# Attention scores of two units at once, computed from 64 rows each, in a sparse-attention, Mamba and FFN kernel

## The reference

```
scores = einsum('bhqd,bhkd->bhqk', Q, K) * scale
mask   = causal & ((cols >= rows - 31) | ((rows - cols) % 64 == 0))
out    = einsum('bhqk,bhkd->bhqd', softmax(where(mask, scores, -inf)), V)
```

## Time and profile before

| | us |
|---|---|
| Median of 3 runs (809.6 to 815.29) | 811.17 |
| The profiled execution | 811.52 |
| Its span, from first to last instruction | 809.7 |
| TensorE busy | 721.4 (89%) |
| VectorE busy | 695.3 (86%) |
| GpSimd busy | 664.2 (82%) |
| ScalarE busy | 594.8 (73%) |

### The profile page before, as it was taken

The page is one execution under the profiler, slowest core; times in us unless marked ns, Lnnn a source line. Parts: engine busy times, 40 slices in busy tenths (PEclk is TensorE's granted clock), DMA queues, the critical chain, the costliest instruction groups (busy, mean ns, idle before and its releaser), DMA issues. The chain is left out here.

```text
span 809.7 us, 22189 instructions
## 1 busy us (share of the span) xinstructions
PE 721.4 (89%) x7840; PEld 430.6 (53%) x7840; DVE 695.3 (86%) x1187; ACT 594.8 (73%) x1161; POOL 664.2 (82%) x824
## 2 busy tenths in 40 slices
PE   5999988998789999998999999899896889897887
PEld 3765655644455447545555456355452356453566
DVE  6977229999999989999889999999998989799983
ACT  5776698797788989887689978868667744764533
POOL 5143437998899989989999799899998999999961
PEclk9999999999999999999999999999999999998999
DMA  5000019888799668877777889889797899898950
GB/s 200 3 3 2 2 54 269 226 231 229 206 225 237 159 173 238 230 177 200 198 213 197 225 233 243 232 230 244 207 253 199 252 259 240 215 266 235 264 158 27
DMA packets 84177, 154.94 MB, mean 191 GB/s; under 512 B 9433, under 2 KB 10082, under 8 KB 84066
## 3 DMA queue, kind: packets, MB, share of 16 engines
q1 hardware_dynamic: 84066, 153.51, 71.4%
HBM read 142.46 MB, written 11.01 MB: 190 GB/s over the span
## 5 line engine op out<-in xcount | busy, mean ns | idle before, releaser
L1779 POOL TENSOR_TENSOR d<-d,cr 128x1024 f32<-128x1024 f32 x128 | 300.0, 2354 | 13.8 <-DVE d L1279 4.1
L1578 ACT ACTIVATE ps<-dt,An 128x512 f32<-128x512 f32 x256 | 173.7, 690 | 71.9 <-DVE d L1279 60.5
L1279 DVE TENSOR_TENSOR_SCAN d<-ps,hl,d 128x512 f32<-128x512 f32 x128 | 157.0, 1262 | 3.7 <-ACT ps L1578 3.3
L1279 DVE TENSOR_TENSOR_SCAN d<-ps,d 128x512 f32<-128x512 f32 x128 | 149.6, 1202 | 7.2 <-ACT ps L1578 6.5
L1267 DVE TENSOR_TENSOR d<-ps,d 128x512 f32<-128x512 f32 x184 | 118.5, 671 | 7.1 <-DMA d<-dud 7.1
L891 PE MATMUL ps<-h,w 128*128 128x512 f16 (+1 forms) x512 | 114.3, 373 | 3.5 <-DVE h L1224 2.8
L1766 POOL TENSOR_TENSOR d<-d,br 128x512 f32<-128x512 f32 x72 | 91.5, 1277 | 4.3 <-DMA d<-dud 4.3
L891 PEld LDWEIGHTS ps<-h,w 128*128 128x128 f16 x512 | 46.8, 98 | 70.9 <-DVE h L1224 12.8
L966 PE MATMUL ps<-d,cst 128*32 128x512 f32 x512 | 69.3, 614 | 10.6 <-POOL d L1779 6.4
L1434 ACT COPY pt<-ps 128x512 f32<-128x512 f32 x96 | 53.8, 589 | 13.9 <-PE ps L825 10.6
L825 PE MATMUL ps<-cst,sx 128*128 128x128 f32 x384 | 56.3, 281 | 8.0 <-ACT sx L1427 3.5
(11 more groups left out here) (182 smaller groups left out, 1457.1 us busy)
## 6 DMA issues: line engine op xcount, KB each, us to landing
dt<-dtd SPq DMA_DIRECT2D x256, 256.0 KB, 5.3
d<-dud SPq DMA_DIRECT2D x256, 256.0 KB, 4.8
dtd<-sR SPq DMA_DIRECT2D x16, 256.0 KB, 4.4
dud<-sE SPq DMA_DIRECT2D x16, 256.0 KB, 3.8
X<-in_x SPq DMA_DIRECT2D x8, 256.0 KB, 6.3
br<-bcd SPq DMA_DIRECT2D x8, 256.0 KB
cr<-bcd SPq DMA_DIRECT2D x8, 256.0 KB
out<-X SPq DMA_DIRECT2D x3, 512.0 KB, 5.8
```

The lines of the kernel that those rows point to most:

```text
L1279: eng.tensor_tensor_scan(d, banks[u % NG][:, :], d, hl[:, r:r + 1] if m % 2 else 0.0, ALU.mult, ALU.add).then_inc(v_sc, 1)
L1578: eng.activation(banks[u % NG][:, :], DT[:, u % NT, :], ACT.Exp, scale=An[:, g:g + 1]).then_inc(s_da, 1)
L1779: eng.tensor_tensor(d, d, CR[m % 2][:, :].unsqueeze(1).to_broadcast((128, n, 512)), ALU.mult).then_inc(p_cm, n)
```

## The change

- A far unit is now 8 windows by 8 heads (64 channels) instead of 4 windows by 16 heads. `UNITS` gets a fourth entry `c`, the half of the channels; the number of units stays 24. Far scores are made in pairs as near ones were: `asc_t` runs for even units only and takes two banks.
- A far pair is 32 products of 64 rows by 64 weight columns that stream 64 columns (8 windows, 2 halves `c`, 2 column halves `j`). A near pair is 8 products of 64 rows by 128 weight columns that stream 128 columns, where it was 16 of 64 by 64.
- Each mask product is made from 64 rows: `e4` becomes the sum of two 32-column pieces of the identity, so that each half of its rows holds what all 128 held.
- `KD` holds two copies instead of four, masked by `rmask` (1 where `row // 32 % 2` is the copy's number). They are written by two 128-row operations with a per-row factor instead of four 32-row copies. GpSimd zeroes only the 64 columns of padding, and `vz_p` no longer touches `KD`.
- `ZF`, `apv_t`, `afar_v`, `aown_s`, `asb_t` and `asc_v` follow the new shape of the far unit, with the same numbers of instructions and elements.
- `WARM` has 42 entries with 215 products, where it had 28 with 152. Two entries of 8 and 2 products stand ahead of the two first transposes. By places: below 100000, 13 products (0 before); 100000 to 280000, 56 (14); to 440000, none (none); to 600000, 20 (21); above, 126 (117).
- `PLACES` is new throughout, so the order of all engines changes.

The diff, without the places and without lines that only follow from the new fourth entry of `UNITS`:

```diff
@@ -21,7 +21,7 @@
 
 
 CONST, NCONST = {}, 0
-for _name, _n in (("ident", 128), ("qmask", 4), ("csel", 56), ("one8", 1)):
+for _name, _n in (("ident", 128), ("qmask", 4), ("csel", 56), ("one8", 1), ("rmask", 2)):
     CONST[_name] = (NCONST, _n)
     NCONST += _n
 
@@ -40,6 +40,7 @@
     put("ident", np.eye(128, dtype=np.float32))
     put("qmask", ((p[:, None] // 8 % 4 == np.arange(4)[None, :]) * float(HD) ** -0.5).astype(np.float32))
     put("csel", (np.arange(56)[None, :] == 24 + p[:, None] % 8).astype(np.float32))
+    put("rmask", (p[:, None] // 32 % 2 == np.arange(2)[None, :]).astype(np.float32))
     put("one8", (p == RK).astype(np.float32))
     return out
 
@@ -64,12 +65,7 @@
 
 
 GROUPS = [(1, g) for g in range(4)] + [(0, g) for g in range(4)]
-UNITS = [(kind, g, kk) for kind, g in GROUPS for kk in range(2 if kind else 4)]
-
-
-def near(u):
-
-    return (u - 8) % 4 // 2, u % 2
+UNITS = [(kind, g, kk, c) for kind, g in GROUPS for kk in range(1 if kind else 2) for c in range(2)]
 NU = len(UNITS)
 
 
@@ -149,7 +145,7 @@
     (BATCH_HALVES, 'aln_p aln_s aln_t ano_s aqk_s aqk_t'),
     (GROUPS_OF, 'afar_v aval_s aval_t'),
     (UNITS_OF, 'aown_s apv_t asc_s asc_v atr_s atr_t'),
-    ([(b, u) for b, u in UNITS_OF if u < 8 or u % 2 == 0], 'asc_t'),
+    ([(b, u) for b, u in UNITS_OF if u % 2 == 0], 'asc_t'),
     ([(b, u) for b, u in UNITS_OF if u in SHIFTED_T], 'asb_t'),
     (JOINS, 'aback_v jexp_s jmix_p jout_t jrec_v jsub_p jsum_p jtr_v jx_v'),
...
@@ -747,27 +742,26 @@
                                            aT[:, 64 * m + 32 * s:64 * m + 32 * s + 64], WT[:, 2, :], start=True, stop=True)
                 t.then_inc(t_av, 1)
 
-            def scores(b, u, mk):
-
-                U = NU * b + u
-                bank = bank_of["sc", b, u] = turn((s_exp, U + 1) if u in SHIFTED_T else (v_sub, shifted(b, u, "v") + 1))
-                eng.matmul(bank[:, :], e4[:, :], mk, start=True, stop=False, skip_group_check=True)
-                return bank
-
             def asc_t(b, u):
-                kind, g, kk = UNITS[u]
+
+                kind, g, kk, _ = UNITS[u]
                 U, gi = NU * b + u, group_of(u)
+                nw = 8 if kind else 4
                 if U == 0:
                     eng.wait_ge(v_set, V_SEL)
-                if kind:
-                    bank = scores(b, u, masks[:, 256:288].unsqueeze(1).to_broadcast((128, 16, 32)))
-                else:
-                    kk, _ = near(u)
-                    if g == kk == 0:
-                        mk = masks[:, 0:256].unsqueeze(1).to_broadcast((128, 2, 256))
+                half = [slice(64 * c, 64 * c + 64) for c in range(2)]
+                two = []
+                for c in range(2):
+                    by = (s_exp, U + c + 1) if u + c in SHIFTED_T else (v_sub, shifted(b, u + c, "v") + 1)
+                    bank = bank_of["sc", b, u + c] = turn(by)
+                    if kind:
+                        mk = masks[half[c], 256:288].unsqueeze(1).to_broadcast((64, 16, 32))
+                    elif g == kk == 0:
+                        mk = masks[half[c], 0:256].unsqueeze(1).to_broadcast((64, 2, 256))
                     else:
-                        mk = masks[:, 64:192].unsqueeze(1).to_broadcast((128, 4, 128))
-                    two = [scores(b, u + c, mk) for c in range(2)]
+                        mk = masks[half[c], 64:192].unsqueeze(1).to_broadcast((64, 4, 128))
+                    eng.matmul(bank[:, :], e4[half[c], :], mk, start=True, stop=False, skip_group_check=True)
+                    two.append(bank[:, :].rearrange("p (a w k) -> p a w k", a=2, w=nw))
                 if b == 0:
                     eng.wait_ge(v_aqm, gi + 1)
                 else:
@@ -775,45 +769,39 @@
                 eng.wait_ge(s_aqk, 4 * b + 2)
                 if U == 0:
                     eng.wait_ge(v_akd, 2)
+                if b == 0 and u == 8:
+                    eng.wait_ge(p_set, 2)
+                if kind == 0 and g == 2:
+                    eng.wait_ge(p_kp, b + 1)
                 qm = QM[gi % 2]
-                if kind:
-                    bw = bank[:, :].rearrange("p (a w k) -> p a w k", a=4, w=4)
-                    Ks = KD[:, :, PAD:PAD + T].rearrange("p a (h x) -> p a h x", x=128)
-                    for k in range(4):
-                        m = 8 * g + 4 * kk + k
-                        lq = qm[:, 4 * kk + k, :, :].rearrange("p a n -> p (a n)")
-                        t = eng.matmul(bw[:, :, k, :].rearrange("p a (h x) -> p a h x", x=4), lq, Ks[:, :, :, 4 * m:4 * m + 4], start=False,
-                                       stop=(k == 3 and u not in SHIFTED_T), skip_group_check=True)
-                    t.then_inc(t_sc, 1)
-                    return
-                if g == 2:
-                    eng.wait_ge(p_kp, b + 1)
-
-                for k in range(4):
-                    m = 8 * g + 4 * kk + k
-                    at = 64 * (m % 16) + m // 16
+                Ks = KD[:, :, PAD:PAD + T].rearrange("p a (h x) -> p a h x", x=128)
+                for k in range(nw):
+                    wi = nw * kk + k
+                    m = 8 * g + wi
                     for c in range(2):
-                        r = slice(64 * c, 64 * c + 64)
-                        for j in range(2):
-                            o = slice(64 * j, 64 * j + 64)
-                            lq = qm[r, 4 * kk + k, 2 * j:2 * j + 2, :].rearrange("p a n -> p (a n)")
-                            dst = two[c][o, :].rearrange("p (a w k) -> p a w k", a=2, w=4)[:, :, k, :]
-                            t = eng.matmul(dst, lq, KD[r, 2 * c:2 * c + 2, at:at + 127:2], start=False,
-                                           stop=(k == 3 and u + c not in SHIFTED_T), skip_group_check=True)
-                        if k == 3:
+                        end = k == nw - 1 and u + c not in SHIFTED_T
+                        if kind:
+                            for j in half:
+                                lq = qm[half[c], wi, j.start // 32:j.stop // 32, :].rearrange("p a n -> p (a n)")
+                                t = eng.matmul(two[c][j, :, k, :].rearrange("p a (h x) -> p a h x", x=4), lq, Ks[half[c], :, :, 4 * m:4 * m + 4],
+                                               start=False, stop=end, skip_group_check=True)
+                        else:
+                            at = 64 * (m % 16) + m // 16
+                            lq = qm[half[c], wi, :, :].rearrange("p a n -> p (a n)")
+                            t = eng.matmul(two[c][:, :, k, :], lq, KD[half[c], :, at:at + 127:2], start=False, stop=end, skip_group_check=True)
+                        if k == nw - 1:
                             t.then_inc(t_sc, 1)
 
...
             def atr_t(b, u):
@@ -826,26 +814,21 @@
                 t.then_inc(t_at, 1)
 
             def apv_t(b, u):
-                kind, g, kk = UNITS[u]
+                kind, g, kk, c = UNITS[u]
                 U, gi = NU * b + u, group_of(u)
+                nw = 8 if kind else 4
                 V, pt = (V1, V2)[kind][g % 2], PT[U % 2]
                 eng.wait_ge(s_av, 8 * b + gi + 1)
                 eng.wait_ge(s_pt, U + 1)
                 bank = bank_of["pv", b, u] = turn((s_own, U + 1))
-                if kind:
-                    bo = bank[:, 0:144].rearrange("p (w a n) -> p w a n", w=4, a=4)
-                    for a in range(4):
-                        for j in range(4):
-                            t = eng.matmul(bo[32 * j:32 * j + 32, :, a, :], pt[:, a, 32 * j:32 * j + 32], V[:, kk, :, 4 * a + j, :], start=True, stop=True)
-                else:
-
-                    kk, c = near(u)
-                    bo = bank[:, 0:72].rearrange("p (w a n) -> p w a n", w=4, a=2)
-                    for i in range(4):
-                        a, w = i // 2, i % 2
-                        for j in range(4):
-                            t = eng.matmul(bo[32 * j:32 * j + 32, 2 * w:2 * w + 2, a, :], pt[:, i, 32 * j:32 * j + 32],
-                                           V[:, 2 * kk + w, :, 4 * (2 * c + a) + j, :], start=True, stop=True)
+                bo = bank[:, 0:18 * nw].rearrange("p (w a n) -> p w a n", w=nw, a=2)
+
+                for i in range(4):
+                    a, w = i // 2, i % 2
+                    at = slice(nw // 2 * w, nw // 2 * w + nw // 2)
+                    for j in range(4):
+                        t = eng.matmul(bo[32 * j:32 * j + 32, at, a, :], pt[:, i, 32 * j:32 * j + 32],
+                                       V[:, 2 * kk + w, :, 4 * (2 * c + a) + j, :], start=True, stop=True)
                 t.then_inc(t_pv, 1)
 
             def jout_t(b, g):
...
@@ -1048,7 +1031,7 @@
             eng.tensor_copy(masks[:, :], mraw0).then_inc(v_set, 2)
             eng.wait_ge(l_w1, 16)
             for k in range(4):
-                eng.tensor_copy(e4[:, 32 * k:32 * k + 32], ident[:, 0:32]).then_inc(v_set, 2 if k == 3 else 1)
```

(20 more changed lines are left out.)

246 lines of the change are left out of this document (121 added, 125 removed), and 321 rows, old and new, of tables (PLACES, WARM).

## The result

The changed kernel takes **820.33 us** (median of 4 runs, 819.21 to 821.72) beside 810.5 us (4 runs) for the kernel before on the same chip: ratio 1.0098, 95% interval 1.0057 to 1.0138 (the quotient of the two medians is 1.012, inside that interval). The forecast was 802, the range ended at 817. The profiled execution took 819.21 us, its span is 817.4 (809.7 before), so the span grew by 7.7 us.

A forecast was written before the change was run, and what follows sets the result against it. It took TensorE to set the pace from 20 to 100 us, VectorE as nearest full to 640, GpSimd afterwards. 811.5 - 1.7 (start) - 3.7 (batch 0) - 3.5 (batches 1 to 3) - 0.4 (key copies) = 802.2, forecast 802; range 789 to 817.

The forecast's parts named there:

- Near scores: Near pairs on TensorE: two 64-row masks stream together, no gain in products; -0.21 us a pair, 32 pairs, -6.7 us.
- Far scores: Far pairs on TensorE: narrower products in quicker rounds, 1.5 us a pair; -0.7 us a pair, 16 pairs, -11.2 us.
- The start: Query and key products before the first scores: early idle products bring the faster clock sooner; -1.7 us.
- Batch 0, -3.7 us: Attention before the first scan, where TensorE sets the pace: most of 4.5 us saved there shortens the run.
- the order: New places of steps on all engines: most stay within some 3 scans; cost 0, give or take 7 us.
- Key copies, -0.4: ScalarE's writing of KD in batches 1 to 3: -1.1 us x 6, of which 0.4 us shows.
- Batches 1 to 3, -3.5 us: Attention woven into the scans: a quarter of the 13.4 us saved on scores there passes on.
- Idle products at 0, up to +5: More idle products on TensorE: 126 added instructions, 14 us of its time, cost the run 0, up to +5 us.
- A: Rival: VectorE keeps the pace, TensorE's savings after 100 us become its idle time; 807 to 808 us, chance 0.22.
- B: Rival: narrow far products run no faster than wide ones, rounds of 0.12 us; 808 us, chance 0.10.
- C: Rival, slower: far pairs hold two of four score banks, so TensorE's queue stands at masks; 817 us, chance 0.11.
- D: Rival, slower: new order puts GpSimd work into the nearly full stretch from 640 us; 815 us, chance 0.12.

The follow-up runs named there:

- e13: The kernel before with 64-row masks in near pairs only, far masks kept at 128 rows; 813.2 us, ratio 0.9995.
- e12: The kernel before with 64-row masks alone, in near pairs and far units; 816.2 us, ratio 1.0044.
- e1: The changed kernel's new steps in the order and with the idle products of the kernel before, five far pairs split; 818.7 us, ratio 1.0067.
- e10: The changed kernel without its first three entries of idle products (11 products); 818.4 us, ratio 1.0062.
- e2: As e1, plus the 8 and 2 idle products ahead of the first two transposes; 821.1 us, ratio 1.0103.
- e9: The changed kernel without the 56 idle products in places 90000 to 280000; 822.7 us, ratio 1.0124.
- e11: The kernel before without any of its 152 idle products; 828.4 us, ratio 1.0193.
- e4: As a run, not the buffer: the changed kernel without the 202 idle products placed above 100000; 830.2 us, ratio 1.0198.
- e7: As e1, with mask products issued again to give TensorE back the work taken away; 829.0 us, ratio 1.0180.

## Why the prediction was wrong

**Near scores: the masks right, the gain twice as large.** Asked for were 1.4 us a pair and overlapping masks. The changed kernel, a near pair and the next, and a far pair:

```profile
16.86 0.39 PE L763 MATMUL ps<-masks,e 64*128 64x512 bf16 x2
17.18 1.16 PE L786 MATMUL ps<-KD,qm 64*64 64x64 f32 x64
18.27 1.12 PE L804 MATMUL ps<-zf,cst 128*128 128x512 f32 x2
...
186.74 0.39 PE L763 MATMUL ps<-masks,e 64*128 64x512 bf16 x2
186.97 1.08 PE L791 MATMUL ps<-KD,qm 64*128 64x128 f32 x16
187.88 0.38 PE L763 MATMUL ps<-masks,e 64*128 64x512 bf16 x2
```

Two masks in 0.23 us, the pair in 1.14: -0.45 for the forecast -0.21, outside its bounds (0 to -0.3). 0.20 of it is the masks (e13). The rest is a turn that is gone, 0.09, since 64x128 masks now stand ahead of 64x128 products, and the products themselves, 0.91 us for 1.07, where the text counted no gain; why 16 of them are quicker than 32 narrower ones is not shown.

**Far scores: right.** 1.41 us for the forecast 1.5, with 64 products in 1.09, 0.017 apart (the text drew the line at 0.03). The turn of 0.09 us that I took from the earlier trace rows is there again: 16.86 to 17.18 is 0.32, 186.74 to 186.97 is 0.23, and e12 shows it between its far masks and scores. The Trainium skill, "TensorEngine Tiling (Array Packing)", section Tiling Modes, says that a change of mode drains the engine; the rows agree, at 0.09 us each. By the rows a near pair gives 0.45 and a far pair 0.81, 27 us in all for the 18 forecast, and the groups above have 28. In e1 the profile has 14.6 us less work; there masks and scores take 84.7 us for the 77.0 of the changed kernel, which has no split pairs.

**The start: right in place, wrong in worth.** 3.70 us for 3.5, first scores at 15.77 for 16.1. Part of the gain was chance: without early idle products the same products took 5.02 us before, but 4.26 in e13 and 4.31 in e1. It stood in the sum with -1.7 us for the end. e10, without the lead, is not slower, and e2, with it, is not quicker than e1.

**Batch 0, -3.7 us: this step failed.** The text said "here TensorE sets the pace", from 39.9 busy us of 40, and that a microsecond is "worth nearly one" there. With the start, the first scan should have come 5.4 us earlier, and it came 0.2 later. The table of leads shows three causes.

First, less work passes on in part only: 0.7 of 1.6 us over the near pairs in e13, 1.1 of 3.6 in e1. The one delay that can be read by itself passes on in full. The changed kernel and e9 are the same program up to the place 100000, but only the changed one has a hole of 0.94 us in a far pair, with no semaphore as the cause; e9 is about 1 us ahead from there to the end of the first FFN:

```profile
24.79 0.93 PE L786 MATMUL ps<-KD,qm 64*64 64x64 f32 x48
26.66 0.46 PE L786 MATMUL ps<-KD,qm 64*64 64x64 f32 x16 [0.94 <-issue]
```

```profile
24.89 1.23 PE L609 MATMUL ps<-KD,qm 64*64 64x64 f32 x64
```

Second, that hole itself. Without it the lead at the first `jx_v` is 3.5 us, so batch 0 had won 1.5 beyond the start by then, and the hole took 1.0 back.

Third, the order, which stood in the sum with 0. From the first `jx_v` to the first FFN in `X` the kernel before takes 22.73 us and the changed one 24.89. One small GpSimd operation of the FFN's layer norm takes 1.86 us instead of 0.20, and TensorE waits for what follows from it. Before, then changed:

```profile
67.53 0.20 POOL L1598 TENSOR_SCALAR frs<-fmv 128x4 f32<-128x4 f32 x1 [1.71 <-DVE fmv L1033]
```

```profile
65.01 1.86 POOL L1576 TENSOR_SCALAR frs<-fmv 128x4 f32<-128x4 f32 x1 [3.61 <-DVE fmv L1016]
...
69.56 0.63 PE L851 MATMUL ps<-cst,lnf 128*128 128x128 f32 x4 [1.62 <-POOL lnf L1585]
```

It is so in all six kernels with the new order (1.83 to 1.86 us, and 24.9 to 25.2 from `jx_v` to FFN) and in none of the nine with the old one (0.20; 22.4 to 22.8). In the old order GpSimd scales a block of layer norm (`lna`) just ahead of it, in the new one it doesn't. Why the operation is then slower is open.

The text had a bound of 0 beside the step, and the choice of the upper end was a mistake. The larger one was to take a lead at the first scan for a gain at the end: e9 is 1.7 us ahead there and 11.4 behind at scan 254, and e13's lead of 1.7 is 1.5 us of lag at scan 64 and 0.9 of lead at scan 254.

**Key copies, -0.4.** ScalarE's two copies take 0.75 us each, 1.50 per batch half for 2.47: 1.0 saved for the forecast 1.1. What it was worth is not separate from the rest.

**Batches 1 to 3, -3.5 us.** The share of a quarter was about right for plain savings: e13 gets 1.6 of 6.3 us at the same clock, e11 3.8 of 37.8, a tenth, give or take 4. In the changed kernel even that does not show, where the order changed as well and 126 instructions of idle products came in.

**Idle products at 0, up to +5.** They were sized at 14 us of TensorE and take 20. Their time doesn't pass one for one, and without the late ones the clock is lower. What they cost net in the changed kernel is not separate from the order; taking out the middle ones changes it by less than the error.

**What was missing: the clock.** No term stood for it, though it is the largest. The mean clock fell from 0.985 to 0.973, and at 4.5 us for 0.01 that is 5.5 of the 6.8 us between the means of the table; 1.4 are left for steps and order together (3.4 against the four runs of before on its own chip, if their clock was 0.985 too). In the profiled executions the parts are work -6.9, clock +12.4, idle +2.3. The rows that could have warned me are the clock of the earlier trace rows: 0.97 in 160 to 220 us, where TensorE had 9 idle us in 60. That the clock fell because TensorE had less to do is not shown: e11, e4 and e9, with less work, have a lower clock, but e7 has as much work as before and 0.974, and e1 without that work 0.975. The Trainium skill, "TensorE: Matmul & The Clock Gate", section Terms, prices lower-clock time at half its length. Here 0.01 of mean clock is 16 us at the lower level, 8 us by that rule, and the runs show 4.5: a bit more than half of it shows in the time.

**The rivals.** A had the mechanism, TensorE's savings become idle time, but gave 807 to 808 with its gains at the start and in batch 0, which are not there either. B fell: the narrow products are the quickest part. C fell for the changed kernel: the idle time ahead of the masks is 2.2 us, 4.2 before. In the old order it has a case, the 1.22 us of e1 at 26.58, and the idle time ahead of the masks is 6.5 us there and 7.7 in e7. D had the place right but not the cause: the last 5.6 us are lost from scan 208 on, but GpSimd is busy 55.7 us in 640 to 700 and 45.4 in 700 to 750, less than the 57.0 of the earlier trace rows and the 47.4 of this window of before:

```profile
700.00:750.00 50.00, 42.18 (x249) 23.84 (x248) 46.61 (x70) 26.91 (x47) 47.40 (x42) 0.93 0.90 252
```

So GpSimd did not become the bound there; all engines got on more slowly, TensorE at 0.90 for 0.93. "A longer stretch after the first scan than 680 us" came true with 687.4.

**Open.** Why this order has more idle times of TensorE of 1.5 us and over than the old one (11 in the changed kernel, 8 before, the start left out) is a matter of 3,300 places that no single run took apart. The holes at 26.7 and 197 us are not explained: at the second a block of TensorE's instructions is fetched (198.67, 1.2 us long), but the hole lasts until 201.3, and the kernel before has 1.18 us at the same step. That the clock causes the slope, and not some third thing that lowers the clock and lengthens the run together, is not shown by a run that changed the clock alone; e4 and e11 speak for it, because they took work away and got slower; e7, whose clock did not come back with its work, leaves open what lowers it.

## What to carry to other kernels

An engine that is busy all the time in a stretch can pass on every delay and still only a part of a saving; try it once with work taken away and once with work put in, and follow a few named steps down the stretch instead of busy time. Where TensorE has a second clock level, a sum of removed work needs a term for the clock, and two kernels should be compared at the same mean clock before a gain or loss is given to the edit. An order that was worked out for one set of durations can cost 3% with another, so a part of such a change tested in the wrong order says little about the part.

## What the runs showed of the hardware

- Pairs of 64-row masks stream side by side: two of 512 columns in 0.23 us, where one of 128 rows takes 0.22.
- 64 products of 64 rows by 64 columns that stream 64 columns take 1.09 us, 0.017 us each, four at once in rounds of 0.068; 32 that stream 128 take 1.07 (e13).
- A turn between array forms costs 0.09 us, and it also comes between a 64x128 mask and 128x128 products (e12), where the whole far unit takes 0.20 us more than with a mask of 128 rows.
- The same `TENSOR_SCALAR` of 128x4 on GpSimd takes 0.20 us in one order of its engine and 1.83 to 1.86 in another, at the same place in six kernels.
- One program's mean clock differs from run to run by 0.016 (e1: 0.965 to 0.981), and its time by 11 us with it (825.06 to 813.85). A handful of executions does not fix a difference of 1% unless the clocks are compared too.
